# Offsets in 32-row by 64-column tiles, two chunks together in four PSUM banks and three phases, without x1b

## The reference

```
x = x + _L0_conv_ref(_gn(x), ...)   # depthwise 3x3, then three 32x32 channel mixes (two through a softmax)
x = x + _L1_conv_ref(_gn(x), ...)

def _L1_conv_ref(x, w_off, w_conv, b_conv):
    off = conv3x3(x, w_off)              # 32 -> 64: a row and a column offset for each channel and pixel
    rows, cols = clip(off + grid)        # then a bilinear sample of x at (rows, cols), channel by channel
    vals_t = fr * (v_rt - v_lt) + v_lt
    vals_b = fr * (v_rb - v_lb) + v_lb
    mapped = fc * (vals_b - vals_t) + vals_t
    return conv3x3(mapped, w_conv) + b_conv
```

## Time and profile before

| | |
|---|---|
| median of 3 runs | 724.89 us (723.59 to 725.79) |
| span of the profiled execution | 724.3 us |
| mean granted TensorE clock | 0.988 |
| PE busy | 95% |
| DVE busy | 72% |
| POOL busy | 66% |
| ACT busy | 64% |
| moved by DMA | 115.64 MB |

### The profile page before, as it was taken

The page is one execution under the profiler, slowest core; times in us unless marked ns, Lnnn a source line. Parts: engine busy times, 40 slices in busy tenths (PEclk is TensorE's granted clock), DMA queues, the critical chain, the costliest instruction groups (busy, mean ns, idle before and its releaser), DMA issues.

```text
span 724.3 us, 10746 instructions
## 1 busy us (share of the span) xinstructions
PE 684.9 (95%) x3500; PEld 244.5 (34%) x3500; DVE 525.0 (72%) x1037; ACT 465.9 (64%) x809; POOL 478.0 (66%) x413
## 2 busy tenths in 40 slices
PE   4799979999999699999999999999999999999986
PEld 4333333333333233333333333333333333333322
DVE  3587988779935858657985598657984775578892
ACT  7487777676728824766567666577656775577860
POOL 4004867888594844868758666886658668787760
PEclk9999999999999989999999999999999999999999
DMA  8958927889459895699948997599957626477555
GB/s 140 186 109 149 136 60 164 174 178 205 121 129 247 163 199 131 157 223 173 201 108 194 200 219 163 132 231 179 207 132 173 158 60 143 116 163 179 123 126 135
DMA packets 140189, 115.64 MB, mean 160 GB/s; under 512 B 15168, under 2 KB 114016, under 8 KB 140128
## 3 DMA queue, kind: packets, MB, share of 16 engines
q1 hardware_dynamic: 116096, 103.12, 68.2%
q10 hardware_dynamic: 24032, 11.78, 9.0%
HBM read 31.59 MB, written 16.78 MB: 67 GB/s over the span
## 4 chain that ended last, share of the span: by engine, by line
PE 61%; SPq 11%; DVE 4%; ACT 3%; POOL 3%; issue 2%; DMA 2%; DVEq 0%; POOLq 0%; ACTq 0%
PE off_ps L781 30%; PE c_ps L670 26%; SPq L388 3%; SPq L469 3%; PE c_ps L681 2%; PE c_ps L685 2%; SPq L451 2%; DMA mapb<-mapa 1%; SPq L420 1%; DVE other_row L1422 1%; ACT other_row L975 1%; ACT off_abs L988 1%; POOL row_diff L1199 1%; SPq L461 1%; PE c_ps L689 1%
## 5 line engine op out<-in xcount | busy, mean ns | idle before, releaser
L1422 DVE COPY_PREDICATED other_row<-down_ps,row_diff 128x768 f32<-128x768 int32 x128 | 124.7, 1027 | 114.8 <-ACT down_ps L986 114.8
L781 PE MATMUL off_ps<-x1a,wo 128*64 128x512 f32 x768 | 176.8, 594 | 0.8 <-DVE other_row L1434 0.8
L781 PE MATMUL off_ps<-x1b,wo 128*64 128x512 f32 x768 | 176.1, 592 | 0.0
L670 PE MATMUL c_ps<-xb,w 128*64 128x512 f32 x336 | 149.8, 593 | 4.2 <-DVE xb L1495 2.0
L670 PE MATMUL c_ps<-mapb,w 128*64 128x512 f32 x336 | 150.8, 594 | 1.6 <-DVE x1a L1407 1.6
L672 PE MATMUL c_ps<-xa,w 128*64 128x512 f32 x336 | 149.8, 593 | 0.0
L975 ACT ACTIVATE other_row<-row_diff 128x768 f32<-128x768 f32 x128 | 100.8, 835 | 67.4 <-POOL row_diff L1201 46.5
L1216 POOL TENSOR_TENSOR other_row<-other_row,x_strips 128x512 f32<-128x512 f32 x48 | 57.2, 1192 | 128.1 <-DVE other_row L1434 128.1
L672 PE MATMUL c_ps<-mapa,w 128*64 128x512 f32 x294 | 131.7, 594 | 0.0
L986 ACT ACTIVATE down_ps<-off_ps,bias_o 128x512 f32<-128x512 f32 x64 | 41.9, 655 | 108.0 <-PE off_ps L781 100.5
L1217 POOL TENSOR_TENSOR other_col<-other_col,other_row 128x512 f32<-128x512 f32 x64 | 86.3, 1349 | 31.4 <-DVE other_row L1434 31.3
(11 more groups left out here) (135 smaller groups left out, 990.3 us busy)
## 6 DMA issues: line engine op xcount, KB each, us to landing
mapa<-mapped SPq DMA_DIRECT2D x224, 65.0 KB, 2.0
x1b<-x1a SPq DMA_DIRECT2D x28, 520.0 KB, 6.5
mapb<-mapa SPq DMA_DIRECT2D x28, 520.0 KB, 8.3
out_dram<-x1a SPq DMA_DIRECT2D x49, 256.0 KB, 4.7
xb<-in_x_dram SPq DMA_DIRECT2D x48, 256.0 KB, 9.0
xa<-in_x_dram ACTq DMA_DIRECT2D x40, 256.0 KB, 7.3
x_strips<-x1a SPq DMA_DIRECT2D x112, 81.2 KB, 2.1
x_strips<-x1a SPq DMA_DIRECT2D x112, 65.0 KB, 2.1
```

What stands on the lines that cost most here:

```text
L670: nc.tensor.matmul(bank[0:64, :], weights[:, kx, :], rows_b[:, of, kx:kx + W], start=(kx == 0), stop=(kx == 2))
L781: last = nc.tensor.matmul(off_ps[k % 2][64 * t:64 * t + 64, CH * n:CH * n + CH], wo[wpar][:, kx, side:side + 2 * C], rows[:, b:b + 7:2, kx ...
L1422: last = dve.copy_predicated(other_row[n][:, :, KR // 2 * odd:KR // 2 * odd + KR // 2, :], bass.AP(tensor=rows.tensor, offset=rows.offset ...
```

## The change

The offset matmuls no longer read two shifted tiles with 128 contracting rows. Each reads one row class (32 partitions) of `x1a` and one tap's 32 x 64 weights, so `x1b` and its copies, on ACT in image 0 and on SP later, are gone. `wo` holds all nine taps for each row class. Two chunks are computed together (a pair u, four in an image). Output row r of four has its own bank, so `off_ps[0]` and `off_ps[1]` (four banks) are filled by one pair. The three kernel rows ky are three phases of 24 matmuls; between phases the row class that writes a bank changes, and each phase waits until the one before is done (`off_phases`). The masks get two banks of their own (`mask_ps`), so `c_ps` has two banks in place of three. A pair's first phase waits for `col_mask_ready` of both chunks of the pair before. The jobs of both chunks stand behind the second phase (the first conv group and what is before it) and behind the third (the others). DVE multiplies with `off_abs`, in one product over both halves. Chunks are numbered so that a pair is the left and the right half of the same rows. ACT, DVE and POOL are reordered by pairs.

```diff
-    def offsets(wpar, par, k):
-        side = 2 * C * (k // 2 % 2)
-        for n, rows in enumerate((x1a[par], x1b)):
-            for kx in range(3):
+    def offsets_phase(wpar, par, u, ky):
+        for kx in range(3):
+            for r in range(4):
+                q = slice(Q * ((r + ky) % 4), Q * ((r + ky) % 4) + Q)
                 for t in range(2):
-                    b = 2 * NJ * t + NJ * (k // 4) + k % 2
-                    last = nc.tensor.matmul(off_ps[k % 2][64 * t:64 * t + 64, CH * n:CH * n + CH],
-                                            wo[wpar][:, kx, side:side + 2 * C],
-                                            rows[:, b:b + 7:2, kx:kx + W],
-                                            start=(kx == 0), stop=(kx == 2))
-        last.then_inc(off_done, 1)
+                    b = 2 * NJ * t + NJ * (u // 2) + u % 2 + (r + ky) // 4
+                    last = nc.tensor.matmul(off_ps[r % 2][64 * t:64 * t + 64, CH * (r // 2):CH * (r // 2) + CH],
+                                            wo[wpar][q, 3 * ky + kx, :], x1a[par][q, b:b + 7:2, kx:kx + W],
+                                            start=(ky == 0 and kx == 0), stop=(ky == 2 and kx == 2))
+        last.then_inc(off_phases, 1)
...
+    def pair_jobs(i, u):
+        behind, n = [[], [], []], 1
+        for job in jobs_behind(i, 2 * u) + jobs_behind(i, 2 * u + 1):
+            behind[n].append(job)
+            if job[0] in ("x1", "c2"):
+                n = min(n + 1, 2)
+        return behind
...
+ (PE)      for u in range(NP):
+               if NP * i + u >= 1:
+                   pe.wait_ge(col_mask_ready, NK * i + 2 * u)
+               for ky, jobs in enumerate(pair_jobs(i, u)):
+                   if NP * i + u >= 1 or ky >= 1:
+                       pe.wait_ge(off_phases, PHASES * (NP * i + u) + ky)
+                   offsets_phase(i % 2, i % 3, u, ky)
+                   for job in jobs:
+                       job_of(job)
...
+ (ACT)         if i == 0 and u == FURTHER_BIAS[0] // 2:
+                   pad_x(i + 2, i % 2)
+               copy_rows(i, e)
+               for job in behind[0] + behind[1]:
+                   evacuate(job)
+               act.wait_ge(off_phases, PHASES * (NP * i + u + 1))
+               row_mask(i, e); lengths(i, e); col_mask(i, e); lengths(i, o)
+               for job in behind[2][:1]:
+                   evacuate(job)
+               row_mask(i, o); col_mask(i, o)
+               copy_rows(i, o)
+               if nxt and u and ("x1", i + 1, 7) in sum(pair_jobs(i, u - 1), []):
+                   pad_x1(i + 1, (i + 1) % 3)
+               if after and i and u == NP - 1:
+                   pad_x(i + 2, i % 2)
+               if nxt and u == NP - 1:
+                   clamp(i + 1, 0)
+               for job in behind[2][1:]:
+                   evacuate(job)
+               sum_far(i, e); sum_far(i, o)
...
+ (DVE)         for job in behind[0] + behind[1]:
+                   follow(job)
+               deform(i, e)
+               for job in behind[2]:
+                   follow(job)
+               if after and u == (2 if i else 1):
+                   x_stats(i + 2, 0)
+               deform(i, o)
+               if nxt and ("x1", i + 1, 7) in sum(behind, []):
+                   x1_norm(i + 1, (i + 1) % 2, (i + 1) % 3)
+               if after and u == (2 if i else 1):
+                   x_stats(i + 2, 1)
+                   x_norm(i + 2, i % 2)
```

More of the change, by code:

```diff
@@ L610, in _ @@
                     wait_apart(x1_pads, v + 1)
-                    for half in range(2):
-                        copy_x1b(0, half)
                     wait_apart(conv2_done, 8 * v)
@@ L888, in pad_x1 @@
                 last = fill(x1a[par][0:Q, 0, 1:W + 1], mean[0:Q, :])
-                if isinstance(i, int) and i == 0:
-                    fill(x1b[3 * Q:P, BL - 1, 1:W + 1], mean[3 * Q:P, :])
-                    last = fill(x1b[:, :, 0:WP:WP - 1], mean[:, :])
                 last.then_inc(x1_pads, 1)
@@ L1060, in _ @@
                         pad_mapped(i, i % 3, 0)
[L1061 to L1063 removed]
+                        clamp(i, 1)
+                    if u == 2:
                         pad_mapped(i, i % 3, 1)
[L1065 to L1069 removed]
@@ L1077, in _ @@
+                    if not nxt and u == 1:
+                        pad_end(i % 3)
+                    if after and i and u == NP - 1:
+                        pad_x(i + 2, i % 2)
+                    if nxt and u == NP - 1:
+                        clamp(i + 1, 0)
+                    for job in behind[2][1:]:
+                        evacuate(job)
+                    sum_far(i, e)
+                    sum_far(i, o)
                     for half in range(2):
-                        if prev and i + 2 < NB and 4 * half + 3 in groups:
+                        if prev and after and 4 * half + 3 in groups:
@@ L1439, in bank @@
             def bank(*job):
-                return c_ps[place[job] % 3]
+                return c_ps[place[job] % 2]
             for half in range(2):
@@ L1460, in _, with follow @@
                 x1_stats(1, 1, m)
+            def follow(job):
+                kind, i, m = job
+                if kind == "x1":
+                    x1_stats(i, i % 3, m)
+                elif kind == "c2":
+                    add_group(i, i % 2, i % 3, m, bank(*job))
             for i in range(NB):
                 prev, nxt, after = i >= 1, i + 1 < NB, i + 2 < NB
-                for k in range(NK):
-                    if nxt and k and 7 in conv1_groups(i, k - 1):
-                        x1_norm(i + 1, (i + 1) % 2, (i + 1) % 3)
-                    if k == (CONV2_SETUP if nxt else END_SETUP) and prev:
+                for u in range(NP):
+                    e, o = 2 * u, 2 * u + 1
+                    behind = pair_jobs(i, u)
+                    if prev and u == (CONV2_SETUP if nxt else END_SETUP) // 2:
@@ L1479, in _ @@
-                    if prev:
-                        for m in (LAST_CONV2 if nxt else END_CONV2)[k]:
-                            add_group(i - 1, (i - 1) % 2, (i - 1) % 3, m, bank("c2", i - 1, m))
-                    if after and k == (4 if i else 1):
+                    for job in behind[0] + behind[1]:
+                        follow(job)
+                    deform(i, e)
+                    for job in behind[2]:
+                        follow(job)
+                    if not nxt and u == END_BIAS // 2:
+                        prepare_conv2(i, i % 2, i % 3)
```

351 lines of the change are left out of this document (148 added, 203 removed).

## The result

The changed kernel takes 777.37 us in the median of four runs (773.91 to 779.01), the kernel before 725.23 beside it: a ratio of 1.07, 95% interval 1.0652 to 1.0747, so 6.5 to 7.5% slower. I had said 779. The profiled execution, the fastest of the four, spans 772.1 us, 47.8 more than before.

The account below looks back on a forecast made before the run. PE, busy 684.9 of 724.3 us, was taken as the bound. To that span came +31 (first image), +22.5 (images 2 to 6) and +0.5 (last image and end), 778.3; forecast 779 us, range 722 to 818.

Parts of the forecast that it names:

- some 35 us higher: Whole forecast, if four row tiles gave the skill's 3.07x and each offset phase took 0.8 us more.
- 0.3: Offset matmuls on PE: the second phase must see the first done, about 0.3 us.
- T: End of a pair's third offset phase on PE, forecast 10.8 us after the pair's start with one group between.
- near 600: Sign in the profile after: PE busy near 600 us, with stalls at the first image's pair starts.
- +31: First image: the first P comes at 206 against 174.75, with 1 us for the clock, +31 us.
- +22.5: Images 2 to 6, SP's loop: five periods of 89 us for 84.5, +22.5 us.
- P: The start of an image's first strips on SP; P to P was 84.5 us before, forecast 89.
- the next image starts at P + 19: Images 2 to 6: the next image starts at P + 19, where before it started at P + 30.6.
- 3 us only: One set of offset banks: with PE's groups as cover, DVE may be late by 3 us only; an x_norm takes 5.4.
- L: Theory on record: SP's queue, through the store of two images back, sets the distance P to P.
- B: Rival: faster, the queues keep ahead; 717 us, or 660 with all waits hidden; chance 0.10.
- D: Rival: row tiles don't run eight at once; at four, 7.7 us more a pair, some 900 us and more; chance 0.08.

Follow-up runs that it names:

- early_pads: Changed kernel with ACT's pad_x1 of the next image earlier, image 1's clamp and first copies behind its first masks, POOL's row differences behind chunk 7: 759.01 us, 1.0477.
- first_image_again: norm_after_selects with another order of image 0 on DVE and ACT and of its jobs behind the phases: 740.53 us, 1.0199.
- store_first: Changed kernel with SP issuing the first-half store of image i-1 ahead of move_mapa of the first half: 769.47 us, 1.0627.
- three orders changed: Changed kernel with early_pads, store_first and adds_earlier together: 752.5 us, 1.0389.
- adds_earlier: Changed kernel with DVE's order changed in images 1 to 6: conv2's second add ahead of chunk 4's deform, group 4's add ahead of x_norm: 779.73 us, 1.0763.
- before_two_banks: The kernel before the change with conv1 and conv2 in two banks of the three, nothing else changed: 737.79 us, 1.0198.
- two_taps_of_three: Changed kernel without the middle tap of each kernel row, 16 offset matmuls in a phase for 24: 763.96 us, 1.0547.
- norm_after_selects: On top of three orders changed: x_norm between selects of chunks 6 and 7, b1 and pad_x in the next image, group 4's adds back: 744.3 us, 1.0245.
- third_bank: Changed kernel with the masks in two SBUF tiles instead of two PSUM banks, and a third bank for conv1 and conv2: 844.71 us, 1.1656.

## Why the prediction came out as it did

**The matmuls (right).** Eight 32-row tiles do run at once: in the phase at 402.50 eight records begin within 0.04 us, the next eight 0.48 after the first, and from then on eight every 0.43; 18 rounds are 7.7 us a pair and a little more. The Trainium skill ("TensorE: Matmul & The Clock Gate", Part 3, measured speedup) gives 3.07x for four row tiles, from which the prediction estimated a phase 0.8 us longer. The trace does not agree: 2.84 us for six rounds shows nothing of it. (The prediction's "some 35 us higher" has no working: 0.8 us in 96 phases would be 77 us of PE's time, of which waits would have hidden a part that I did not work out.) From the last round of phase 1 to the first of phase 2 the trace has 0.76 us for 0.43, my "0.3". T came 11.3 us after a pair's start (413.79 less 402.50; forecast 10.8). PE's busy time is 657.6, not near 600: stalls brought the 1.2 GHz level, at which records are longer (mean granted clock 0.951 for 0.988). In the last image a stall of 3.98 us was followed by 96 records in 8.39 us for 5.81, and this window, in which the columns are busy times and then the granted clock, shows the level behind the stall at 480.67:

```profile
481.00:484.00 3.00, 3.00 (x10) 0.79 (x8) 2.90 (x5) 0.95 (x2) 0.00 (x0) 0.50 0.48 111
```

**Image 0 and 1 (right, +28.0 for +31).** Pairs 1 to 3 of image 0 and image 1 start at 71.8, 88.3, 112.7 and 133.9; the steps gave 71.5, 87.7, 111.1 and 133.7. ACT waited 11.5 us for the mean and 12.3 for the strips, and chunk 7's `mapped` held the second lengths for 4.1 us; pair 1 of image 1 came at 162.0 (164). early_pads won back 7.7 of the 28 us by order alone and first_image_again 10.0; that the other 18 are order too, no run here shows.

**Images 2 to 6 (the loop right, +12.7 for +22.5, and one step wrong).** The forecast's loop was: the store has landed and ACT evacuates at P + 42.5, the next P comes 45.5 later, and 1 us for the clock, 89. In the trace ACT's wait for that store ends at P + 38.9 to 39.8 in these five images, 39.4 on average, and the next P comes 46.8 to 47.9 later, 47.7 on average: 87.0. So the loop on record does set P to P, 2 us shorter: the store came 3 us earlier than I had it, the way from there to the next strips was 2 longer, and the clock's 1 us was not needed on top. The step that failed is "the next image starts at P + 19". It starts at P + 25.3 to 27.0 (402.5 less 375.6), because pair 3 takes 24 to 26 us: I had costed DVE's lateness at "3 us only" of cover and then given pair 3 none of it. Since the store's end stands fixed to P, that late start does not lengthen the loop; it hides the wait, which is 28.3 us in all, not over 60, and costs pair 0 about 1 us. What I had missed is a second loop of nearly the same length, through DVE's work in pairs 2 and 3: with L's wait removed (store_first) P to P is still 86.1; with three orders changed it is 84.3, and 82.3 where `x_norm` and b1 too have left their place. adds_earlier's 88.7 comes near my 89 by chance: it is 1.6 us longer than the loop that the changed kernel ran.

**Banks (one part right).** ACT's masks held PE's next pair for 24.4 us: 4.9 in image 0, 7.0 in image 1, 12.6 in the last. The dearer half was one that I had named only in passing: two banks for the conv groups, 38.9 us at one line. By before_two_banks they cost 13 us where nothing else is changed. In the changed kernel their share stays open: a third bank beside four for the offsets and two for the masks would be a ninth, and the run that freed one by moving the masks changed DVE's and POOL's work as well. So how much of the 38.9 us is two banks and how much is DVE's lateness by itself is not shown.

**Last image (7.1 for 0.5).** Its start is P + 21.2 for 19, yet T of its pair 2 is P + 66.2 for 65.4. The loss comes in pair 3, whose T is P + 86.8 for 81: PE waits 6.7 us for the masks behind T of pair 2 where I had 4.7, and then needs 13.9 us to T at the lower clock where I had 10.8. For the clock of this whole stretch I had allowed 2 us.

**The rivals.** B, that PE's saving wins, fails: two_taps_of_three takes another 82 us from PE and gets 13. That also says where the 84 us went, as far as the runs show it: the pairs' length is set by chains through ACT, DVE and POOL, which PE's longer work covered before, and PE's own busy time fell by 27 us only (684.9 to 657.6). D, that tiles don't run eight at once, is refuted by the trace. That the forecast came within 2 us of the median is luck: the sum lies only 6.2 us above the span because errors cancelled, 3 us too much in the first images, 9.8 in the middle ones and 6.6 too little at the end; and the median then stood 5.3 us above the span, not 0.6, since the profiled execution was the fastest.

## What to carry to other kernels

Before PE's work is cut in a kernel whose PE is 95% busy, add up for each stretch what DVE, ACT and POOL must do in it, in their order. Their mean shares of 64 to 72% did not show that little of the cut could be had (of a further 82 us, 13 came back); the count for pairs 2 and 3, 41 us of DVE's work for PE's 38.5, pointed to the place where norm_after_selects then won 5.5 us in pair 3. When two loops are within 1 us of each other (87.0 and 86.1 here), removing one shows the other; experiments have to take both away to show what either costs. And a mask moved from PSUM to SBUF does not make a bank for nothing: with the bank that it made it cost 67 us.

## What the runs showed that I had not expected

DVE's predicated copy of 512 takes 0.73 us, and 1.80 when its mask lies in SBUF and POOL is at work (third_bank); POOL's own operation beside it goes from 1.27 to 1.9 us.
